# Reordered sums in the convolution loop and one image fewer in the DRAM round trip of a convolution with batch norm

## The chip, the cores and the metric

One core of one Trainium2 chip runs the whole program. The metric is device time in microseconds (us) of one launch. The kernel before took 1618.82 us, the median of 3 runs (1618.82 to 1619.4).

## The reference

```python
x: (32, 256, 28, 28) float32
xp  = log_pooling(x)            # 12 fixed averages (2 radii x 6 angles) over a 9x9 neighbourhood, laid out 4x3
out = conv(xp, w_conv1, stride (4, 3)) + conv(x, w_center) + b_center
mean, var = out.mean((0, 2, 3)), out.var((0, 2, 3))
out = (out - mean) * rsqrt(var + 1e-5) * gamma + beta
return relu(out + x)
```

The mean and the variance run over all 32 images, so nothing can be finished until every image has been convolved.

## The kernel before

The 256 channels lie as 128 partitions by two halves (c = 0, 1 of the input, o = 0, 1 of the output). An image of y (the convolution's result) is 128 x 1568 float32, 784 KB. Each image goes through two steps s = 2 * image + c. A step makes, on VectorE (DVE), differences of columns, box sums, and "pooled" sums from them. All products are made in three parts (high by high, low by high, high by low): ScalarE (ACT) copies a rounded high part, DVE subtracts it to get the low part (`lo_of_sums`, `lo_of_shifted`, `lo_of_pooled`), and TensorE (PE) multiplies. `inner_split` holds the parts of the inner sums and `pooled_split` those of the three pooled pairs. There is one buffer of each.

The DVE program of a step, in its written order (each engine runs its own program in order):

1. `differences`, which writes the source of `inner_split`. ACT then makes the high parts (`split_inner`).
2. at c = 0 `take_middle` of the image before, which puts the middle products into `y_stage`.
3. `lo_of_sums`, which waits for ACT and which PE waits for at the start of its step (`inner_lo_ready`).
4. `three_columns` (L467, row <- row, x_pad, then row3v <- row), which waits for `row2_ready`.
5. `lo_of_shifted`, `boxes`, at c = 0 `take_y` of the image before (it waits for PE to have finished that image), `first_sum`, `second_sum`, `lo_of_pooled` 0, `third_sum`, `lo_of_pooled` 1 and 2.

`row2` is a sum of two shifted reads of `x_wide`, made by DMAs. SP's queue (L285) loads the first operand as soon as `second_sum` of the step before has freed the buffer. POOL (L248) waits for it to land and issues a DMA that adds the second operand. `ends` is made the same way behind it, and `third_sum` waits for it. In SP's program the store of the last image's y (`y_stage` to `y_dram`, L315) stands behind the two loads at c = 0.

In the very first step SP issues, in this order: x, the first part of the weights, the first operand of `row2`, the second part of the weights (the outer taps); then it waits for the finished `row2`, and then come the first operand of `ends`, the x of c = 1 and the other weights.

The statistics use a pivot near the mean. In image 1 DVE makes it from image 0 with four `bn_stats`, two `bn_aggr` and a product (`make_pivot`). From then on ACT's `measure` takes two sums per half of each image, with the pivot as bias.

The last phase reuses the 191 KB per partition of phase-1 buffers as 30 places of 784 KB. Slot d = 0 is `y_stage` and `x_pad`; slot d > 0 is place 2d - 2 for y and place 2d - 1 for x, so 16 slots and 2 rounds. `tail_image(round_, d)` says which image a slot holds. The image in `y_stage` (LAST = 31) is never stored. All others are stored and loaded again. SP loads the places of round 0 as their old contents die: place 0 before image LAST - 1, places 1 and 2 before image LAST, places 3 to 6 once the y of image LAST - 1 is saved (`y_saved`), 7 to 11 once PE is through c = 0 of the last image, 12 to 21 once the last low parts exist, and so on. Per slot DVE scales and adds x (L710), ACT applies the relu (L459) and issues the store (L462). In round 1 SP and POOL load y and x into a slot once its store has landed.

Of the kernel before, what the change touches and what calls it, by code (L numbers as in the profile page):

```python
# [7 lines left out]
def conv_bn_relu_program(nc, x, x_wide, w_raw, b_center, gamma, beta, out, y_dram):  # L8
# [57 lines left out]
    with ctx:  # L66
        def sb(name, size, dt=F32):
            return ctx.enter_context(nc.sbuf_tensor(name, [P, size], dt))
# [68 lines left out]
        ALL_PLACES = 2 * (SLOTS - 1)  # L137

        def tail_image(round_, d):
            return LAST if round_ == d == 0 else SLOTS * round_ + d - 1  # L140

        def y_slot(d):
            return y_stage[:, :] if d == 0 else view(phase2, 2 * (d - 1) * PLACE, (1, PLACE))
# [8 lines left out]
                return view(x_pad, 2 * H, (X_PAD, CH), (1, HW))  # L152
            return view(phase2, (2 * d - 1) * PLACE, (HW, CH), (1, HW))

        pivot_stats = sb("pivot_stats", CH * 2 * 6)
        pivot_moments = sb("pivot_moments", CH * 2)
        minus_pivot = sb("minus_pivot", CH)
        sums = sb("sums", 2 * CH * IMAGES)
        totals = sb("totals", 2 * CH)
# [118 lines left out]
        def _(sp):  # L278
# [5 lines left out]
            def begin_sum(image, c, buf, n_columns, begun):  # L284
                sp.dma_start(view(buf, 0, (1, n_columns * TALL_PITCH)),  # L285
                             x_wide[bass.ds(image, 1), :, c, 0:n_columns * TALL_PITCH]
                             .rearrange("n p f -> p (n f)")).then_inc(begun, 16)
# [15 lines left out]
            def image_steps(image, first=False, last=False):  # L303
                for c in range(CH):
                    if not last:
                        sp.wait_ge(row3_ready, CH * image + c + 1)
                        sp.wait_ge(v_ready, CH * image + c + 1)
                        load_x(image + 1, c)
                    if c == 0:
                        begin_sums(image, 1)  # L310
                    elif not last:
                        begin_sums(image + 1, 0)
                    if c == 0 and not first:
                        sp.wait_ge(y_ready, CH * image + FREE)
                        sp.dma_start(y_dram[bass.ds(image - 1, 1)].rearrange("n p f -> p (n f)"),  # L315
                                     y_stage[:, :]).then_inc(y_saved, 16)
# [6 lines left out]
                    .then_inc(tail_loaded[d], 16)  # L323

            def load_places(first, end):
                for k in range(first, min(end, ALL_PLACES)):
                    (load_tail_x if k % 2 else load_tail_y)(0, 1 + k // 2)

            load_x(0, 0)
            load_weights(0, 0)  # L330
            begin_sum(0, 0, row2, W + 3, row2_begun)
            load_weights(0, 1)
            sp.wait_ge(row2_ready, 16)
            begin_sum(0, 0, ends, W, ends_begun)
            load_x(0, 1)
            load_weights(1, 0)
            load_weights(1, 1)
# [11 lines left out]
            load_places(1, 3)  # L349
            image_steps(LAST, last=True)  # L350

            sp.wait_ge(y_saved, 16 * LAST)
            load_places(3, AFTER_STAGE)
            sp.wait_ge(pooled_done, PAIRS * (CH * IMAGES - 1))
            load_places(AFTER_STAGE, AFTER_FIRST)
# [17 lines left out]
        def _(act):  # L373
# [28 lines left out]
            def copy_middle(image):  # L402
# [3 lines left out]
                for m in range(2):  # L406
                    nc.scalar.activation(view(m_copy, m * CH * HALF, (HALF, CH), (H, U), (1, H)),
                                         view(acc, (MBANK + CH * m) * BANK, (BANK, CH), (1, U), (U, H)), ACT.Copy)\
                        .then_inc(m_copied, 1)

            def measure(image, o):
                act.wait_ge(y_ready, CH * image + o + 1 + FREE)
                act.wait_ge(pivot_ready, 1)
                for kind, function in enumerate((ACT.Identity, ACT.Square)):
                    wait_from_one(act, y_measured, MOMENTS * image + KINDS * o + kind)
                    nc.scalar.activation(view(m_copy, 0, (1, HW)), view(y_stage, o * HW, (1, HW)), function,  # L416
                                         bias=minus_pivot[:, o:o + 1],
                                         accum_out=sums[:, bass.ds((kind * CH + o) * IMAGES + image, 1)])\
                        .then_inc(y_measured, 1)

            def image_steps(image, first=False, second=False):
                for c in range(CH):
                    s = CH * image + c
                    if c == 0 and not first:
                        copy_middle(image - 1)
                    split_inner(s)
                    if c == 1 and not first and not second:
                        measure(image - 1, 1)
                    if first:
                        split_weights(c, range(len(GROUPS)))  # L430
                        act.wait_ge(warmed_up, 1)
                    for j in range(PAIRS):
                        split_pooled(s, j)
                        if second and c == 1 and j > 0:
                            measure(image - 1, j - 1)
                    if c == 0 and not first and not second:
                        measure(image - 1, 0)

            act.sem_inc(m_copied, FREE)
# [2 lines left out]
            act.wait_ge(zeroed, ZEROED)  # L442
            image_steps(0, first=True)
            image_steps(1, second=True)
            with act.Fori(2, IMAGES) as image:
                image_steps(image)
            copy_middle(LAST)
            for o in range(CH):
                measure(LAST, o)
# [16 lines left out]
        def _(dve):  # L466
# [47 lines left out]

            every_other_column = (2 * H, U), (1, H)

            def take_middle(image):

                dve.wait_ge(m_copied, 2 * image + 2 + FREE)
                wait_from_one(dve, y_saved, 16 * image)  # L520
                wait_from_one(dve, y_measured, MOMENTS * image)
                m1, m2 = (view(m_copy, m * CH * HALF, (HALF, CH), (H, U), (1, H)) for m in range(2))
                add(view(y_stage, 0, (HW, CH), *every_other_column), m2, m1)
                sub(view(y_stage, H, (HW, CH), *every_other_column), m1, m2).then_inc(middle_taken, 1)

            def take_y(image):
                dve.wait_ge(pooled_done, PAIRS * CH * (image + 1))
                dve.wait_ge(middle_taken, image + 1 + FREE)
                for o in range(CH):
                    y = view(y_stage, o * HW, (H, 2), (2 * H, U), (1, H))  # L530
                    add(y, view(acc, 2 * o * BANK, (BANK, 2), (H, U), (1, H)), y).then_inc(y_ready, 1)

            def make_pivot():
                dve.wait_ge(y_ready, CH + FREE)
                for o in range(CH):
                    for half in range(2):
                        link(nc.vector.bn_stats(pivot_stats[:, (2 * o + half) * 6:(2 * o + half + 1) * 6],
                                                y_stage[:, o * HW + half * HALF:o * HW + (half + 1) * HALF]))
                for o in range(CH):
                    link(nc.vector.bn_aggr(pivot_moments[:, 2 * o:2 * o + 2],  # L540
                                           pivot_stats[:, 12 * o:12 * o + 12]))
                nc.vector.tensor_scalar(minus_pivot[:, :], view(pivot_moments, 0, (2, CH)), -1.0, None, ALU.mult)\
                    .then_inc(pivot_ready, 1)


            def pooled_place(s, j, first, *dims):
# [103 lines left out]
            def image_steps(image, second=False):  # L650
                for c in range(CH):
                    s = CH * image + c
                    differences(image, c)
                    if c == 0:
                        take_middle(image - 1)
                    lo_of_sums(s)
                    three_columns(image, c)
                    lo_of_shifted(s)
                    if second and c == 0:
                        take_y(image - 1)  # L660
                    boxes(s)
                    if not second and c == 0:
                        take_y(image - 1)
                    first_sum(s)
                    second_sum(s)
                    lo_of_pooled(s, 0)
                    if second and c == 1:
                        make_pivot()
                    third_sum(s)
                    lo_of_pooled(s, 1)  # L670
                    lo_of_pooled(s, 2)
# [3 lines left out]
            dve.wait_ge(zeroed, ZEROED)  # L675
            first_image()
            image_steps(1, second=True)
            with dve.Fori(2, IMAGES) as image:
                image_steps(image)
            take_middle(LAST)  # L680
            take_y(LAST)

# [4 lines left out]
            link(sub(var[:, :], totals[:, CH:2 * CH], square[:, :]))  # L687
            nc.vector.tensor_scalar(var[:, :], var[:, :], 0.0, EPS, ALU.max, ALU.add).then_inc(var_ready, 1)
            dve.wait_ge(params_loaded, 48)
            dve.wait_ge(pivot_ready, 1)  # L690
            link(sub(mean[:, :], totals[:, 0:CH], minus_pivot[:, :]))
            link(add(mean[:, :], mean[:, :], bias[:, :]))
            link(sub(bn_shift[:, :], bias[:, :], mean[:, :]))
# [10 lines left out]

            for round_ in range(ROUNDS):
                for d in range(SLOTS):
                    wait_from_one(dve, tail_loaded[d], 16 * round_ + 32 * (d > 0))
                    wait_from_one(dve, tail_x_loaded[d], 16 * round_)
                    for o in range(CH):
                        nc.vector.scalar_tensor_tensor(  # L710
                            out=x_slot(d, o), in0=y_slot(d)[:, o * HW:(o + 1) * HW],
                            scalar=bn_scale[:, o:o + 1], in1=x_slot(d, o), op0=ALU.mult, op1=ALU.add)\
                            .then_inc(scaled, 1)
# [108 lines left out]
```

## Time and profile before

| | |
|---|---|
| median of 3 runs | 1618.82 us |
| profiled execution, its own time | 1618.86 us |
| span in the profile, first to last instruction | 1617.2 us |
| TensorE matmul busy | 1461.5 us (90%), 8518 instructions |
| DVE busy | 1443.0 us (89%), 1327 instructions |
| ACT busy | 658.6 us (41%) |
| HBM read / written | 218.07 MB / 50.58 MB |

The page divides the span into 40 slices of 40.4 us. TensorE is full until slice 36 and does nothing after. The DMA engines are between four and seven tenths busy until there, and full to the end. The kernel so has two parts, a convolution paced by the compute engines and a last phase paced by bytes, and a change has to be read in each of them.

### The profile page before, as it was taken

How to read it: one execution, taken by the hardware profiler on the slowest of the kernel's cores; microseconds unless marked ns; L12 is line 12 of the kernel's file. 1: busy time of each engine (PE TensorE's matmuls, PEld its weight loads, DVE VectorE, ACT ScalarE, POOL GpSimd, SP SyncE). 2: the span in 40 equal slices, each digit the busy share in tenths (PEclk: the TensorE clock that was granted, in tenths of full speed). 3: DMA queues.
4: the chain of work that ended last, by engine and by line, in shares of the span. 5: the costliest groups of instructions: out<-in, count | busy, mean ns of one | idle time of the engine just before them, and what ended most of it. 6: DMA issues, size and time to landing. Idle time of an engine off the chain costs nothing.

```text
span 1617.2 us, 22814 instructions
## 1 busy us (share of the span) xinstructions
PE 1461.5 (90%) x8518; PEld 1458.7 (90%) x8518; DVE 1443.0 (89%) x1327; ACT 658.6 (41%) x721; POOL 121.0 (7%) x160
## 2 busy tenths in 40 slices
PE   9999999999999999999999999999999999993000
PEld 9899999999999999999999999999999999993000
DVE  8999999999999999999999999999999999996432
ACT  3334444444333444434343344433434344444432
POOL 1000000000000000000000000000000000000000
PEclk9999999999999999999999999999999999996555
DMA  7355555565455555555545555455554566579999
GB/s 222 88 133 140 144 129 129 131 147 131 122 120 134 147 137 128 127 133 140 131 113 123 145 146 136 125 127 139 137 126 110 132 147 158 155 237 424 425 425 402
DMA packets 65352, 268.76 MB, mean 166 GB/s; under 512 B 7616, under 2 KB 7616, under 8 KB 65344
## 3 DMA queue, kind: packets, MB, share of 16 engines
q1 hardware_dynamic: 39744, 160.53, 30.3%
q0 software_dynamic: 20736, 82.45, 25.7%
q10 hardware_dynamic: 4864, 25.69, 3.8%
q14 instruction: 6, 0.05, 0.0%
q8 instruction: 2, 0.03, 0.0%
HBM read 218.07 MB, written 50.58 MB: 166 GB/s over the span
## 4 chain that ended last, share of the span: by engine, by line
PE 83%; DVE 5%; DMA 4%; ACTq 3%; ACT 3%; issue 1%; SPq 0%; DVEq 0%; POOLq 0%
PE acc L724 28%; PE acc L725 28%; PE acc L723 28%; ACTq L462 3%; ACT phase L459 2%; DMA phase<-y_dram 2%; DVE phase L467 1%; DMA ends<-x_wide 1%; DVE pooled_split L468 1%; DMA row<-x_wide 1%; DMA out<-phase 1%; ACT m_copy L416 0%; DVE y_stage L467 0%; DVE inner_split L468 0%; DVE row L467 0%
## 5 line engine op out<-in xcount | busy, mean ns | idle before, releaser
L398 ACT ACTIVATE pooled_split<-phase 128x1456 fp32r<-128x1456 f32 x192 | 274.1, 1428 | 637.7 <-DVE phase L467 637.2
L468 DVE TENSOR_TENSOR pooled_split<-phase,pooled_split 128x1456 fp32r<-128x1456 f32 x192 | 315.1, 1668 | 0.3 <-ACT pooled_split L398 0.3
L723 PE MATMUL acc<-pooled_split,w_first 128*128 128x364 f32 x768 | 252.3, 329 | 1.5 <-DVE pooled_split L468 1.4
L724 PE MATMUL acc<-pooled_split,w_first 128*128 128x364 f32 x768 | 252.9, 329 | 0.0
L725 PE MATMUL acc<-pooled_split,w_first 128*128 128x364 f32 x768 | 252.8, 329 | 0.0
L725 PE MATMUL acc<-pooled_split,w_outer 128*128 128x364 f32 x768 | 252.7, 329 | 0.0
L723 PE MATMUL acc<-pooled_split,w_outer 128*128 128x364 f32 x768 | 252.1, 328 | 0.5 <-DVE pooled_split L468 0.5
L724 PE MATMUL acc<-pooled_split,w_outer 128*128 128x364 f32 x768 | 252.5, 329 | 0.0
L723 PE MATMUL acc<-inner_split,w_inner 128*128 128x392 f32 (+1 forms) x640 | 216.4, 338 | 3.0 <-DVE w_inner L510 3.0
L723 PE MATMUL acc<-inner_split,w_first 128*128 128x392 f32 (+1 forms) x640 | 217.8, 340 | 0.7 <-DVE inner_split L468 0.5
L725 PE MATMUL acc<-inner_split,w_inner 128*128 128x392 f32 (+1 forms) x640 | 217.3, 340 | 0.0
L724 PE MATMUL acc<-inner_split,w_inner 128*128 128x392 f32 (+1 forms) x640 | 217.3, 339 | 0.0
L724 PE MATMUL acc<-inner_split,w_first 128*128 128x392 f32 (+1 forms) x640 | 216.4, 338 | 0.0
L725 PE MATMUL acc<-inner_split,w_first 128*128 128x392 f32 (+1 forms) x640 | 215.5, 337 | 0.0
L467 DVE TENSOR_TENSOR phase<-box,row 128x1456 f32<-128x1456 f32 x128 | 208.1, 1667 | 0.0
L389 ACT ACTIVATE inner_split<-phase 128x1568 fp32r<-128x1568 f32 x64 | 97.1, 1518 | 208.3 <-DVE phase L467 208.3
L468 DVE TENSOR_TENSOR inner_split<-phase,inner_split 128x1568 fp32r<-128x1568 f32 x64 | 114.4, 1788 | 49.0 <-ACT inner_split L389 49.0
L723 PEld LDWEIGHTS acc<-pooled_split,w_first 128*128 128x128 f32 x768 | 144.4, 188 | 2.5 <-DVE pooled_split L468 2.5
L723 PEld LDWEIGHTS acc<-pooled_split,w_outer 128*128 128x128 f32 x768 | 144.2, 188 | 0.8 <-DVE pooled_split L468 0.8
L724 PEld LDWEIGHTS acc<-pooled_split,w_outer 128*128 128x128 f32 x768 | 144.5, 188 | 0.0
L725 PEld LDWEIGHTS acc<-pooled_split,w_outer 128*128 128x128 f32 x768 | 144.4, 188 | 0.0
L724 PEld LDWEIGHTS acc<-pooled_split,w_first 128*128 128x128 f32 x768 | 144.3, 188 | 0.0
(82 smaller groups left out, 2222.6 us busy)
## 6 DMA issues: line engine op xcount, KB each, us to landing
row<-x_wide SPq DMA_DIRECT2D x64, 558.0 KB, 3.7
row<-x_wide POOLq DMA_DIRECT2D x64, 558.0 KB, 7.5
ends<-x_wide SPq DMA_DIRECT2D x64, 504.0 KB, 3.9
ends<-x_wide POOLq DMA_DIRECT2D x64, 504.0 KB, 6.5
x_pad<-x SPq DMA_DIRECT2D x64, 392.0 KB, 3.1
y_dram<-y_stage SPq DMA_DIRECT2D x31, 784.0 KB, 5.5
phase<-y_dram SPq DMA_DIRECT2D x30, 784.0 KB, 23.6
out<-phase ACTq DMA_DIRECT2D x30, 784.0 KB, 33.3
```

Source lines behind the costliest of these rows:

```text
L389: nc.scalar.activation(view(inner_split, 0, (1, SD)), view(phase2, INNER_LOW, (1, SD)), ACT.Copy)\
L398: nc.scalar.activation(view(pooled_split, 2 * j * PAIR, (1, PAIR)), view(phase2, POOLED_LOW + 2 * j * PAIR, (1, PAIR)), ACT.Copy)\
L459: nc.scalar.activation(x_slot(d, o), x_slot(d, o), ACT.Relu, bias=bn_shift[:, o:o + 1]).then_inc(relu_done, 1)
L462: act.dma_start(out[tail_image(round_, d)].rearrange("p c w h -> p c (w h)"), x_slot_whole(d)).then_inc(stored[d], 16)
L467: add = lambda out_, a, b: nc.vector.tensor_tensor(out_, a, b, ALU.add)
L468: sub = lambda out_, a, b: nc.vector.tensor_tensor(out_, a, b, ALU.subtract)
L723: nc.tensor.matmul(place, hi_w, hi_in, start=start, stop=False)
L724: nc.tensor.matmul(place, lo_w, hi_in, start=False, stop=False)
L725: return nc.tensor.matmul(place, hi_w, lo_in, start=False, stop=stop)
```

## The change

- **Steps with c = 1**, in every image but the first: `three_columns` stands ahead of `lo_of_sums`. At c = 0 the order stays.
- **First step**: SP issues the first operand of `ends` ahead of its wait for `row2`, and the second part of the weights behind that wait.
- **Pivot**: made by ACT with two passes over `y_stage` (identity scaled by -1/784, with the running sum kept) behind the pooled parts of c = 0 of image 1. DVE's `make_pivot` is gone, and image 1 is measured in the same positions as every later image.
- **Image LAST - 1**: its y is finished in place 0 instead of `y_stage`. It is neither stored nor loaded. Slot 1 of round 0 holds it, and image 0 goes to slot 15 of round 1. SP no longer waits for that store ahead of places 3 to 6.
- The image loops of DVE and ACT end one image earlier, and the last image is written out.

```diff
         def tail_image(round_, d):
-            return LAST if round_ == d == 0 else SLOTS * round_ + d - 1
+            if d == 0 and round_ == 0:
+                return LAST
+            if d == 1 and round_ == 0:
+                return LAST - 1
+            return 0 if SLOTS * round_ + d == LAST else SLOTS * round_ + d - 1
...
-                    if c == 0 and not first:
+                    if c == 0 and not first and not last:
                         sp.wait_ge(y_ready, CH * image + FREE)
                         sp.dma_start(y_dram[...], y_stage[:, :]).then_inc(y_saved, 16)
...
-                for k in range(first, min(end, ALL_PLACES)):
+                for k in range(max(first, 1), min(end, ALL_PLACES)):
...
             begin_sum(0, 0, row2, W + 3, row2_begun)
+            begin_sum(0, 0, ends, W, ends_begun)
+            sp.wait_ge(row2_ready, 16)
             load_weights(0, 1)
-            sp.wait_ge(row2_ready, 16)
-            begin_sum(0, 0, ends, W, ends_begun)
             load_x(0, 1)
...
-            sp.wait_ge(y_saved, 16 * LAST)
+            sp.wait_ge(y_saved, 16 * (LAST - 1))
             load_places(3, AFTER_STAGE)
...
+            def make_pivot():            # on ACT
+                for o in range(CH):
+                    act.wait_ge(y_ready, o + 1 + FREE)
+                    wait_from_one(act, pivot_ready, o)
+                    nc.scalar.activation(view(m_copy, 0, (1, HW)), view(y_stage, o * HW, (1, HW)), ACT.Identity,
+                                         scale=-1.0 / HW, accum_out=minus_pivot[:, o:o + 1])\
+                        .then_inc(pivot_ready, 1)
...
+            def y_place(image, first, *dims):
+                if isinstance(image, int) and image == LAST - 1:
+                    return view(phase2, first, *dims)
+                return view(y_stage, first, *dims)
...
                     if c == 0:
                         take_middle(image - 1)
-                    lo_of_sums(s)
-                    three_columns(image, c)
+                        lo_of_sums(s)
+                        three_columns(image, c)
+                    else:
+                        three_columns(image, c)
+                        lo_of_sums(s)
                     lo_of_shifted(s)
...
-                    if second and c == 1:
-                        make_pivot()
...
-            with dve.Fori(2, IMAGES) as image:
+            with dve.Fori(2, LAST) as image:
                 image_steps(image)
+            image_steps(LAST)
```

## Rows read from the trace of the kernel before

**Rows 1.** The page: busy time of TensorE, and what the DMAs moved in 40 slices.

```profile
PE 1461.5 (90%) x8518; PEld 1458.7 (90%) x8518; DVE 1443.0 (89%) x1327; ACT 658.6 (41%) x721; POOL 121.0 (7%) x160
GB/s 222 88 133 140 144 129 129 131 147 131 122 120 134 147 137 128 127 133 140 131 113 123 145 146 136 125 127 139 137 126 110 132 147 158 155 237 424 425 425 402
```

**Rows 2.** Waits: who waited for whom, us in total, times, longest.

```profile
DVE inner_split L468 <- ACT inner_split L389: 49.0, 31, 1.6
DVE y_stage L467 <- PE acc L725: 33.0, 26, 10.5
```

**Rows 3.** Timeline, DVE, image 30: start, duration, [idle before <- releaser].

```profile
1378.47 0.97 DVE L467 TENSOR_TENSOR y_stage<-acc,y_stage 128x784 f32<-128x784 f32 x1 [0.94 <-PE acc L725]
...
1394.67 1.79 DVE L468 TENSOR_TENSOR inner_split<-phase,inner_split 128x1568 fp32r<-128x1568 f32 x1 [1.58 <-ACT inner_split L389]
1396.38 1.03 DVE L467 TENSOR_TENSOR row<-row,x_pad 128x840 f32<-128x840 f32 x1
```

**Rows 4.** Timeline, image 30: SP's store, POOL's row2 addition, PE's first product of c = 1.

```profile
1387.14 0.43 SPq L315 DMA_DIRECT2D y_dram<-y_stage  x1
...
1387.75 0.86 POOL L248 DMA_DIRECT2D row<-x_wide  x1 [19.58 <-DMA row<-x_wide]
...
1400.82 0.34 PE L723 MATMUL acc<-inner_split,w_inner 128*128 128x392 f32 x1
```

**Rows 5.** DMA issues, the addition at 1387.75: KB, us from issue to landing.

```profile
row<-x_wide POOLq DMA_DIRECT2D x1, 558.0 KB, 7.8
```

**Rows 6.** The same at c = 1 of image 2: POOL's issue, its landing, DVE's sum.

```profile
129.35 0.86 POOL L248 DMA_DIRECT2D row<-x_wide  x1 [17.38 <-DMA row<-x_wide]
...
row<-x_wide POOLq DMA_DIRECT2D x1, 558.0 KB, 8.0
...
137.75 1.03 DVE L467 TENSOR_TENSOR row<-row,x_pad 128x840 f32<-128x840 f32 x1
```

**Rows 7.** Timeline, DVE: `take_y` of images 1, 4 and 5.

```profile
119.86 1.85 DVE L467 TENSOR_TENSOR y_stage<-acc,y_stage 128x784 f32<-128x784 f32 x2
...
252.10 1.84 DVE L467 TENSOR_TENSOR y_stage<-acc,y_stage 128x784 f32<-128x784 f32 x2
...
296.55 1.86 DVE L467 TENSOR_TENSOR y_stage<-acc,y_stage 128x784 f32<-128x784 f32 x2 [0.31 <-PE acc L725]
```

**Rows 8.** Timeline, DVE, first step: the third sum.

```profile
27.53 1.74 DVE L467 TENSOR_TENSOR phase<-box,ends 128x728 f32<-128x728 f32 x2 [2.05 <-DMA ends<-x_wide]
```

**Rows 9.** Timeline, image 1: ACT's last pooled part of c = 0, DVE's pivot.

```profile
80.70 1.42 ACT L398 ACTIVATE pooled_split<-phase 128x1456 fp32r<-128x1456 f32 x1 [1.81 <-DVE phase L467]
...
100.03 2.37 DVE L537 BATCH_NORM_STATS2 pivot_stats<-y_stage 128x6 f32<-128x392 f32 x4
...
103.00 1.74 DVE L467 TENSOR_TENSOR phase<-box,ends 128x728 f32<-128x728 f32 x2
...
106.64 1.68 DVE L468 TENSOR_TENSOR pooled_split<-phase,pooled_split 128x1456 fp32r<-128x1456 f32 x1 [0.31 <-ACT pooled_split L398]
```

**Rows 10.** Timeline, image 31: DVE's sum at c = 0, SP's store and loads.

```profile
1418.83 1.03 DVE L467 TENSOR_TENSOR row<-row,x_pad 128x840 f32<-128x840 f32 x1 [1.16 <-DMA row<-x_wide]
...
1423.81 1.85 DVE L467 TENSOR_TENSOR y_stage<-acc,y_stage 128x784 f32<-128x784 f32 x2
...
1432.46 0.43 SPq L315 DMA_DIRECT2D y_dram<-y_stage  x1
1438.20 0.33 SPq L322 DMA_DIRECT2D phase<-x  x1
...
1456.36 0.33 SPq L319 DMA_DIRECT2D phase<-y_dram  x1
```

**Rows 11.** DMA issues: the addition at 1408.99, the load at 1456.36, and the first x.

```profile
row<-x_wide POOLq DMA_DIRECT2D x1, 558.0 KB, 9.8
...
phase<-y_dram SPq DMA_DIRECT2D x1, 784.0 KB, 6.5
...
x_pad<-x SPq DMA_DIRECT2D x1, 392.0 KB, 3.1
```

More of the change, by code:

```diff
@@ L153, in x_slot_whole @@
             return view(phase2, (2 * d - 1) * PLACE, (HW, CH), (1, HW))
-        pivot_stats = sb("pivot_stats", CH * 2 * 6)
-        pivot_moments = sb("pivot_moments", CH * 2)
         minus_pivot = sb("minus_pivot", CH)
@@ L409, in copy_middle @@
                         .then_inc(m_copied, 1)
+            def make_pivot():
[5 more added lines that the diff above has]
+                        .then_inc(pivot_ready, 1)
             def measure(image, o):
                 act.wait_ge(y_ready, CH * image + o + 1 + FREE)
-                act.wait_ge(pivot_ready, 1)
+                act.wait_ge(pivot_ready, CH)
                 for kind, function in enumerate((ACT.Identity, ACT.Square)):
                     wait_from_one(act, y_measured, MOMENTS * image + KINDS * o + kind)
-                    nc.scalar.activation(view(m_copy, 0, (1, HW)), view(y_stage, o * HW, (1, HW)), function,
+                    y = phase2 if isinstance(image, int) and image == LAST - 1 else y_stage
+                    nc.scalar.activation(view(m_copy, 0, (1, HW)), view(y, o * HW, (1, HW)), function,
                                          bias=minus_pivot[:, o:o + 1],
@@ L426, in image_steps @@
                     split_inner(s)
-                    if c == 1 and not first and not second:
+                    if c == 1 and not first:
                         measure(image - 1, 1)
@@ L433, in image_steps @@
                         split_pooled(s, j)
-                        if second and c == 1 and j > 0:
-                            measure(image - 1, j - 1)
-                    if c == 0 and not first and not second:
+                    if second and c == 0:
+                        make_pivot()
+                    if c == 0 and not first:
                         measure(image - 1, 0)
@@ L444, in _ @@
             image_steps(1, second=True)
-            with act.Fori(2, IMAGES) as image:
+            with act.Fori(2, LAST) as image:
                 image_steps(image)
+            image_steps(LAST)
             copy_middle(LAST)
@@ L515, in _ @@
             every_other_column = (2 * H, U), (1, H)
+            def y_place(image, first, *dims):
+                if isinstance(image, int) and image == LAST - 1:
+                    return view(phase2, first, *dims)
+                return view(y_stage, first, *dims)
             def take_middle(image):
                 dve.wait_ge(m_copied, 2 * image + 2 + FREE)
-                wait_from_one(dve, y_saved, 16 * image)
+                if isinstance(image, int) and image == LAST:
+                    dve.wait_ge(y_saved, 16 * (LAST - 1))
+                elif not (isinstance(image, int) and image == LAST - 1):
+                    wait_from_one(dve, y_saved, 16 * image)
                 wait_from_one(dve, y_measured, MOMENTS * image)
                 m1, m2 = (view(m_copy, m * CH * HALF, (HALF, CH), (H, U), (1, H)) for m in range(2))
-                add(view(y_stage, 0, (HW, CH), *every_other_column), m2, m1)
-                sub(view(y_stage, H, (HW, CH), *every_other_column), m1, m2).then_inc(middle_taken, 1)
+                add(y_place(image, 0, (HW, CH), *every_other_column), m2, m1)
+                sub(y_place(image, H, (HW, CH), *every_other_column), m1, m2).then_inc(middle_taken, 1)
             def take_y(image):
@@ L529, in take_y @@
                 for o in range(CH):
-                    y = view(y_stage, o * HW, (H, 2), (2 * H, U), (1, H))
+                    y = y_place(image, o * HW, (H, 2), (2 * H, U), (1, H))
                     add(y, view(acc, 2 * o * BANK, (BANK, 2), (H, U), (1, H)), y).then_inc(y_ready, 1)
[L533 to L543, printed above, removed]
             def pooled_place(s, j, first, *dims):
@@ L677, in _ @@
             image_steps(1, second=True)
-            with dve.Fori(2, IMAGES) as image:
+            with dve.Fori(2, LAST) as image:
                 image_steps(image)
+            image_steps(LAST)
             take_middle(LAST)
@@ L689, in _ @@
             dve.wait_ge(params_loaded, 48)
-            dve.wait_ge(pivot_ready, 1)
+            dve.wait_ge(pivot_ready, CH)
             link(sub(mean[:, :], totals[:, 0:CH], minus_pivot[:, :]))
@@ L706, in _ @@
                 for d in range(SLOTS):
-                    wait_from_one(dve, tail_loaded[d], 16 * round_ + 32 * (d > 0))
+                    wait_from_one(dve, tail_loaded[d], 16 * round_ + 32 * (d > 0) - 16 * (d == 1))
                     wait_from_one(dve, tail_x_loaded[d], 16 * round_)
```

## The prediction

> **What bounds the kernel now.** I read the page first, then the waits, then the timeline of one late image. On the page TensorE is busy for 1461.5 us, and the DMAs move 110 to 158 GB/s until slice 35, 237 in the next and 402 to 425 to the end [rows 1]. So two things are asked of each edit: whether it moves the convolution, which ends in slice 36, and whether it moves bytes in the stretch in which the DMAs are full. The waits say that DVE is nearly as loaded as TensorE. It waits for TensorE in only 26 places, and 31 times it waits 1.6 us for ACT's rounded copy [rows 2]. The timeline shows both in image 30: 0.94 us for TensorE ahead of `take_y`, 1.58 us for ACT ahead of `lo_of_sums` at c = 1 [rows 3]. `take_y` comes every 45.08 us from image 5 to image 29's end ((1378.47 - 296.55) / 24) [rows 3, 7]. That is TensorE's pace. From image 1 to 4 DVE didn't wait for TensorE and took 44.08 us an image ((252.10 - 119.86) / 3) [rows 7]; in the late images it is 45.08 - 0.94 = 44.14. I take 44.12 as DVE's own pace. **DVE has about 0.96 us an image to spare, and the change touches exactly that.**
>
> **The new order at c = 1.** It is meant to fill the 1.58 us wait with `three_columns`. But `three_columns` needs `row2`, and that arrives late. In image 30 POOL issues the addition at 1387.75 and it lands 7.8 us later, at 1395.55 [rows 4, 5]. The differences are done at about 1394.67 - 1.58 = 1393.09. DVE's sum started at 1396.38, so it had 0.83 us of margin [rows 3]. In image 2 it is 129.35 + 8.0 = 137.35 against 137.75, a margin of 0.40 [rows 6]. I read all 29 images from 2 to 30 this way, and the mean margin is 0.575 us. Moved ahead, the sum can start only that much earlier (less 0.04 us for the release). The 1.71 us of `lo_of_sums` (1396.38 - 1394.67), which lay inside the wait for the addition, now stands behind it. The chain that feeds the addition (`second_sum`, SP's load, POOL, landing) hangs on DVE's own work a fixed distance ahead, so it doesn't get faster. DVE then takes 44.12 + 1.71 - 0.575 + 0.04 = **45.29 us an image against TensorE's 45.08**: it becomes the bound, by 0.21 us an image. What is queued behind DVE's new wait is all of the step: both low parts, the boxes, and all that ACT, SP and POOL do from them. TensorE waits for the first low part, which it took up at 1400.82 when it had been there since 1396.4 [rows 3, 4], 4.4 us early. In the new order it would be there at 1396.38 - 0.79 + 2.0 (the two sums of `three_columns`, 1.03 us the first) + 1.71 = 1399.3, so 1.5 us of cover are left, and DVE's growing lag uses them up. Bounds: 44.08 and a landing 0.1 us earlier give 45.15, 44.14 and one 0.1 later give 45.41. Over 29 images that is +2.0 to +9.6 us, +6.1 at my value.
>
> **First step.** DVE waits 2.05 us for `ends` [rows 8]. The load of `ends` now goes out behind that of `row2`, some 12 us earlier, and its addition right behind `row2`'s on POOL, so the wait should go: -2.05 us for DVE. The outer weights go out about 12 us later instead. They cover themselves if they land before ACT's first pooled copy; if not, they give the 2.05 back. Range -2.05 to 0; I take -2.05, as these weights are 768 KB and head SP's queue when it wakes.
>
> **Pivot.** DVE loses 103.00 - 100.03 = 2.97 us of work and a 0.31 us wait for ACT, whose measuring stood in the way: -3.28 us [rows 9]. ACT gets two passes (about 1 us each) and measures c = 0 behind them. It ends its last pooled copy of c = 0 at 82.1 and has nothing to do for some 5 us, so about 4.3 us of passes fit. Cost 0. DVE paces from there, so both savings count.
>
> **DVE's chain to the last image.** `take_y` of image 1: 119.86 - 2.05 - 3.28 + 1.17 (the new order in image 1) = 115.70. 29 images of 45.29 lead to 1429.1. At c = 0 of the last image the addition is 1.16 us late because two loads of places go out ahead of it [rows 10]. Before, that fell into the time to spare; now it counts: 1430.3 against 1423.81 [rows 10], a shift of **+6.5 us**. All later releases hang on DVE, so the DMA phase begins that much later.
>
> **Bytes.** One store and one load of 784 KB are gone. The load (place 0) lay before the full stretch and is worth nothing. The store lay at its start, 1432.46 [rows 10]. It is worth 0.803 MB / 425 GB/s = **-1.9 us** [rows 1]. Slot 1 needs no y, and image 0 in the last slot needs what image 30 needed: 0. The bound from below is 0 and from above 3.8, if both counted.
>
> **What the missing wait lets loose.** SP's wait for that store held places 3 to 6 back from 1432.46 to 1438.20 [rows 10]. Now four loads go out at once, ahead of the last `row2` addition. With one store ahead the addition lands in 7.8 us, with two loads in 9.8 [rows 5, 11]. With four I take 10.8, between 9.8 and 13.8 (2 us for each more). In times of before, it is then issued at 1432.46 + 0.61 = 1433.07 [rows 4, 10], lands at 1443.9 instead of letting the sum start at 1441.7 (1396.38 + 45.34), and with 1.71 us of `lo_of_sums` behind it the last low parts are 3.9 us later: places 12 and up are released at 1460.3 instead of 1456.36. The load released there landed 6.5 us later, at 1462.9, behind others [rows 10, 11]; without the store the queue would bring it at 1461.0. But a load of 784 KB needs at least 3.1 + 0.9 = 4.0 us [rows 11] and so lands at 1464.3. The DMAs stand idle for **+3.3 us** (range 0 to 6).
>
> The Trainium skill ("DMA: Bandwidth & Descriptors", Queues, rings and completion order) says that each DMA engine takes turns between the queues' rings packet by packet. By that rule the POOL queue's addition gets its turns however many of SP's loads are queued, the landing would stay near the 9.8 us of the two-load case, and the idle time would be 2.3 us and not 3.3. The one-store and two-load rows differ by 2.0 us for 1.9 us of bytes and don't decide it.
>
> **The sum**, against the profiled execution's own 1618.86 us (its span of 1617.2 and 1.7 around it; the median of the runs shown is 1618.82): 1618.86 + 6.5 - 1.9 + 3.3 = **1626.8 us**, 0.5% slower.
>
> **Rivals.**
> - *The reorder pays and TensorE stays the bound.* If the addition at c = 1 lands early enough that DVE stays under 45.08 us, the convolution gains at its start alone, about 2.05 us, and the DMAs 1.9: 1618.86 - 2.05 - 1.9 = 1614.9 us, 0.2% faster, if the DMAs don't stand idle, and 1618.2 if they do for 3.3 us. It decides where the landing at c = 1 comes 0.2 us earlier than read. Against it: the 29 landings have a mean margin of 0.575 us, and it would take 0.8. For it: single images have that (image 30: 0.83 [rows 3 to 5]).
> - *A draw.* DVE's pace is 45.15 and the DMAs stand idle for 1 us: +2.4 - 1.9 + 1 = 1620.4, within 1615.6 to 1622.1. For it: 0.1 us of landing is 2.9 us of time.
> - *Worse.* Landings grow by 0.2 us and four loads hold the addition for 13.8 us: +12 - 1.9 + 6 = 1635.
> - *The tail edit does nothing.* If other DMAs hide the store, the -1.9 falls away: 1628.7. It lies inside the forecast's case.
>
> **How the numbers follow.** A difference of 0.2% is about what a measurement of this kernel can tell from none. Forecast (1622.1 to 1632.5) 0.62; reorder pays 0.17, of which 0.03 end within 0.2%; draw 0.17; worse 0.04. The range takes in the first three nearly whole: 1614.5 to 1632.5. Faster 0.14, same 0.20, slower 0.66.
>
> **What would show it.** Right: DVE waits at L467 row <- row, x_pad for the DMA 31 times for some 2.8 us each and no more for ACT at c = 1; the spacing of `take_y` is 45.2 to 45.4 us; TensorE has some 25 short waits for DVE's `inner_split`; DVE's waits for TensorE at `take_y` are gone but the last; no pivot and no wait at 27.5; DMA idle near the release of places 12 and up. Wrong: a spacing of 45.08 with waits for TensorE left; a landing of the c = 1 addition well under 7.8 us; first pooled copy of ACT late behind the outer weights.

## The result, and the profile after

The changed kernel takes **1626.26 us**, the median of 6 runs (1623.81 to 1628.43), against 1619.09 (1618.82 to 1619.53) for the kernel before on the same chips: a ratio of 1.0040, 95% interval 1.0029 to 1.0051. The forecast was 1626.8. The profiled execution has a span of 1625.0 us against 1617.2.

The page of the changed kernel: busy time, and GB/s in 40 slices.

```profile
PE 1466.1 (90%) x8518; PEld 1460.2 (90%) x8518; DVE 1438.1 (88%) x1320; ACT 660.3 (41%) x725; POOL 121.3 (7%) x160
GB/s 221 95 126 147 137 136 124 127 147 137 123 113 131 147 137 127 126 133 147 130 119 120 135 146 135 125 124 139 141 127 111 129 143 140 157 243 380 425 424 405
```

DVE has 4.9 us less to do than before and the kernel is slower all the same. The full stretch of the DMAs starts later: slice 37 moves 380 GB/s and not 424 [rows 1]. The waits say why.

```profile
DVE row L481 <- DMA row<-x_wide: 89.2, 32, 5.1
...
DVE y_stage L481 <- PE acc L738: 10.5, 2, 10.2
PEld acc L736 <- DVE inner_split L482: 10.3, 12, 3.7
```

The 31 waits for ACT are gone, and so are the waits for TensorE at `take_y`, 33.0 us in 26 places before [rows 2]: two are left, one of them at the very end. In their place DVE waits 32 times for the `row2` addition. Without the longest (5.07 us) and the one at c = 0 of the last image (1.06) that is (89.2 - 5.07 - 1.06) / 30 = 2.77 us each, where the wait for ACT took 1.58. And TensorE now waits for DVE. Image 30 on the timeline, with the landing of its addition (issued at 1392.82):

```profile
1400.89 1.03 DVE L481 TENSOR_TENSOR row<-row,x_pad 128x840 f32<-128x840 f32 x1 [2.79 <-DMA row<-x_wide]
...
1402.94 1.78 DVE L482 TENSOR_TENSOR inner_split<-phase,inner_split 128x1568 fp32r<-128x1568 f32 x1
...
row<-x_wide POOLq DMA_DIRECT2D x1, 558.0 KB, 8.0
```

The addition landed at about 1400.8 and DVE started right behind it; `lo_of_sums` stands behind the sums. `take_y` of images 1, 29 and 30, the lines that answer to [rows 3], [rows 7] and [rows 10]:

```profile
116.01 1.86 DVE L481 TENSOR_TENSOR y_stage<-acc,y_stage 128x784 f32<-128x784 f32 x2 [0.32 <-PE acc L738]
...
1383.49 1.85 DVE L481 TENSOR_TENSOR y_stage<-acc,y_stage 128x784 f32<-128x784 f32 x2
...
1429.93 1.85 DVE L481 TENSOR_TENSOR phase<-acc,phase 128x784 f32<-128x784 f32 x2
```

(1383.49 - 116.01) / 28 = **45.27 us an image**, against the 45.08 that the kernel before kept from image 5 on. The last image, DVE's and SP's timeline and the last addition's landing (issued at 1439.27):

```profile
1438.58 0.43 SPq L325 DMA_DIRECT2D phase<-x  x1
...
1449.60 1.03 DVE L481 TENSOR_TENSOR row<-row,x_pad 128x840 f32<-128x840 f32 x1 [5.07 <-DMA row<-x_wide]
...
1465.97 0.33 SPq L322 DMA_DIRECT2D phase<-y_dram  x1
...
row<-x_wide POOLq DMA_DIRECT2D x1, 558.0 KB, 10.2
```

The four loads that no longer wait for a store go out from 1438.58. Two are issued ahead of the addition (1438.58 and 1439.06) and two behind it (1439.53 and 1440.42), and the addition takes 10.2 us. Places 12 and up are released at 1465.97. That is 36.0 us behind `take_y` of image 30, against 1456.36 - 1423.81 = 32.6 before [rows 10]. The windows of 1 us there, with TensorE, PEld, DVE, ACT, POOL, granted clock, DMA share and GB/s:

```profile
1463.00:1464.00 1.00, 1.00 (x8) 1.00 (x7) 1.00 (x1) 1.00 (x1) 0.00 (x0) 1.00 0.84 351
1464.00:1465.00 1.00, 1.00 (x8) 1.00 (x7) 1.00 (x2) 1.00 (x3) 0.00 (x0) 1.00 0.00 0
1465.00:1466.00 1.00, 1.00 (x7) 1.00 (x7) 1.00 (x2) 0.66 (x1) 0.00 (x0) 1.00 0.00 0
1466.00:1467.00 1.00, 1.00 (x8) 1.00 (x7) 1.00 (x2) 0.00 (x0) 0.00 (x0) 1.00 0.32 44
1467.00:1468.00 1.00, 1.00 (x8) 1.00 (x7) 0.72 (x1) 0.00 (x0) 0.00 (x0) 1.00 0.61 125
```

The DMAs lose 0.16 + 1 + 1 + 0.68 + 0.39 = 3.2 us of a stretch that must be full. The kernel before has no such gap: its DMAs move 425 GB/s around its release at 1456.36.

A measure that splits each span in two helps from here on: **the lead** is the start of `take_y` of image 30, and **the tail** is the rest of the span. A kernel's lead shows the convolution's pace, its tail the DMA phase. Both are of the profiled execution. The kernel before took 1618.94 us beside e1 to e4, 1618.99 beside e5, e6, e8 and e9, and 1618.56 beside e7; the ratios are to these. A ratio is estimated from all runs of both kernels and can differ by 0.0005 from the quotient of the medians.

| kernel | lead | tail | median | ratio to before, 95% interval |
|---|---|---|---|---|
| before | 1423.8 | 193.4 | 1619.09 | |
| changed | 1429.9 | 195.1 | 1626.26 | 1.0040 (1.0029 to 1.0051) |
| e1 changed, old order | 1419.7 | 193.2 | 1614.62 | 0.9973 (0.9962 to 0.9983) |
| e2 before, new order alone | 1436.7 | 193.3 | 1631.56 | 1.0077 (1.0063 to 1.0091) |
| e3 changed, late store | 1421.1 | 195.0 | 1617.78 | 0.9993 (0.9984 to 1.0002) |
| e4 changed, late loads | 1431.1 | 193.4 | 1626.75 | 1.0043 (1.0030 to 1.0057) |
| e5 before, `ends` first alone | 1422.7 | 193.4 | 1616.76 | 0.9987 (0.9978 to 0.9996) |
| e6 old order, late loads | 1419.9 | 192.5 | 1613.99 | 0.9968 (0.9956 to 0.9980) |
| e7 late store, late loads | 1419.9 | 192.0 | 1614.28 | 0.9974 (0.9963 to 0.9984) |
| e8 before, pivot on ACT alone | 1421.5 | 193.1 | 1617.07 | 0.9987 (0.9978 to 0.9996) |
| e9 old order, early loads | 1419.1 | 192.4 | 1613.15 | 0.9963 (0.9950 to 0.9977) |

### The profile page after: what moved, and what is told of

It reads as the page before. It is cut to its first block, busy times and chain, and to the rows that moved or that the text cites. A ratio compares the mean times of both kernels' runs of the same rounds, so it can differ in the third digit from the quotient of the medians.

```text
span 1625.0 us, 22771 instructions
## 1 busy us (share of the span) xinstructions
PE 1466.1 (90%) x8518; PEld 1460.2 (90%) x8518; DVE 1438.1 (88%) x1320; ACT 660.3 (41%) x725; POOL 121.3 (7%) x160
## 4 chain that ended last, share of the span: by engine, by line
DVE 37%; DMA 19%; PE 18%; issue 16%; ACT 4%; ACTq 4%; DVEq 1%; POOLq 0%; SPq 0%
DMA row<-x_wide 19%; DVE phase L481 11%; DVE inner_split L482 7%; PE acc L736 6%; PE acc L737 6%; PE acc L738 6%; DVE box L481 4%; ACTq L476 4%; ACT phase L473 3%; DVE row L481 3%; DVE y_stage L481 3%; DVE pooled_split L482 3%; DVE d L482 2%; DVE phase L482 1%; DVE y_stage L482 1%
## 5 line engine op out<-in xcount | busy, mean ns | idle before, releaser
L481 DVE TENSOR_TENSOR row<-row,x_pad 128x840 f32<-128x840 f32 x64 | 66.0, 1031 | 89.2 <-DMA row<-x_wide 89.2
```

Source lines behind the costliest of these rows:

```text
L481: add = lambda out_, a, b: nc.vector.tensor_tensor(out_, a, b, ALU.add)
```

## The experiments

The theory is that of the prediction: the new order puts `lo_of_sums` behind a DMA that lands late. Its main rival is that something else in the change costs the time.

**e1, the old order back in the changed kernel.**

```diff
                     if c == 0:
                         take_middle(image - 1)
-                        lo_of_sums(s)
-                        three_columns(image, c)
-                    else:
-                        three_columns(image, c)
-                        lo_of_sums(s)
+                    lo_of_sums(s)
+                    three_columns(image, c)
```

> The changed kernel with lo_of_sums ahead of three_columns again at c = 1; all else as changed. Theory (the new order makes DVE the bound because row2 lands late): the spacing of take_y goes back to 45.08 us with waits for TensorE of some 0.9 us, DVE waits for ACT 1.58 us at c = 1. TensorE ends image 1 some 3.5 us earlier than in the kernel before, the store saves 1.9, and the DMAs' idle time shrinks from 3 us to some 1.6, because the last low parts no longer stand behind a sum: 1615 us (1613 to 1618). Rival (the loss comes from something else in the change, such as the written-out last image or the pivot on ACT): it stays at 1624 to 1628 us.

Measured 1614.62 us. The waits of this kernel:

```profile
DVE inner_split L482 <- ACT inner_split L392: 49.1, 31, 1.6
...
DVE y_stage L481 <- PE acc L735: 30.7, 26, 8.5
```

The 31 waits for ACT are back, and so are those for TensorE; the spacing is 45.08 us again. One edit is worth 11.6 us, more than the whole change costs. The rest of the change is a gain of 0.27%. The idle time of the DMAs isn't gone with the order: places 12 and up are released at 1453.93, 34.3 us behind `take_y` of image 30, where it was 32.6 before, and the 6 us from 1452 on move 282 GB/s.

**e2, the new order alone in the kernel before** (the same lines, the other way round).

> The kernel before with three_columns ahead of lo_of_sums at c = 1, and nothing else. Theory: DVE takes 45.27 us an image from image 1 on, without the 2.05 and 3.28 us that the changed kernel saves at its start: take_y of image 30 comes at 119.9 + 1.2 + 29 * 45.27 + 1.2 = 1435 instead of 1423.8, so 1630 us (1627 to 1634). Rival (the new order is harmless alone): 1619 us.

Measured 1631.56 us, 0.8% slower than before. Its waits:

```profile
DVE row L467 <- DMA row<-x_wide: 87.4, 32, 3.5
...
PEld acc L726 <- DVE inner_split L468: 12.1, 17, 2.7
```

The spacing is (1390.12 - 122.11) / 28 = 45.29 us. The new order costs 12.6 us here and 11.6 in the changed kernel, so it doesn't need the other edits to do harm. e1 and e2 together leave the rival nothing.

**e3, the store of y moved behind the addition**, to test that it is the landing which sets the pace.

```diff
                         load_x(image + 1, c)
+                    if c == 1 and not first and not last:
+                        sp.wait_ge(y_ready, CH * image + FREE)
+                        sp.dma_start(y_dram[...], y_stage[:, :]).then_inc(y_saved, 16)
                     if c == 0:
                         begin_sums(image, 1)
                     elif not last:
                         begin_sums(image + 1, 0)
-                    if c == 0 and not first and not last:
-                        sp.wait_ge(y_ready, CH * image + FREE)
-                        sp.dma_start(y_dram[...], y_stage[:, :]).then_inc(y_saved, 16)
```

> The changed kernel with SP's store of the last image's y moved from c = 0, where it goes out just ahead of POOL's row2 addition for c = 1, to c = 1 behind the load of the next x. The new order at c = 1 stays. Theory (the landing of the addition sets DVE's pace, and 1.5 us of it is the store ahead of it): the landing at c = 1 falls from 7.7 us to the 6.2 us of c = 0, DVE's wait from 2.75 to some 1.3 us, DVE's own pace to 43.8 us, and TensorE is the bound again at 45.08: 1616 us (1614 to 1619), the 3 us of idle DMAs being left. Rival (the landing doesn't depend on the store): the pace stays at 45.27 us and the time at 1624 to 1628 us.

Measured 1617.78 us. Waits, DVE's sum in image 30 and the landing of its addition (issued at 1384.85):

```profile
DVE row L481 <- DMA row<-x_wide: 49.8, 32, 5.0
...
DVE y_stage L481 <- PE acc L738: 34.7, 28, 8.6
...
1391.59 1.03 DVE L481 TENSOR_TENSOR row<-row,x_pad 128x840 f32<-128x840 f32 x1 [1.54 <-DMA row<-x_wide]
...
row<-x_wide POOLq DMA_DIRECT2D x1, 558.0 KB, 6.7
```

The mean landing at c = 1 (images 2 to 30) falls from 7.82 to 6.50 us, the wait with it, and TensorE is the bound again at 45.08 us, with the new order in place. So the new order costs this much because the addition lands when it does, and 1.3 us of that is the store ahead of it. It still gains nothing: the time is 1.8 us over what was expected and 3.2 over e1, which has the old order. The lead is 1.4 us longer than in e1. One part of that is a wait of 1.07 us of TensorE for the low part of c = 1 in image 1, which e1 doesn't have. The tail, 195.0, keeps all that the changed kernel lost there.

**e4, the four loads held back in the changed kernel.**

```diff
             sp.wait_ge(y_saved, 16 * (LAST - 1))
+            sp.wait_ge(row2_ready, 16 * CH * IMAGES)
             load_places(3, AFTER_STAGE)
```

> The changed kernel in which SP waits for the last row2 addition ahead of places 3 to 6. Theory (these four loads hold the addition up for some 4 us, and the last low parts with it): the addition lands in 6.3 us instead of 10.2, TensorE's wait of 3.4 us there and the 3 us without DMA traffic ahead of places 12 and up go; about 1 us of DMA time is lost ahead of the four loads: 1624 us, 2 us under the changed kernel (1622 to 1625). Rival (the idle time lies elsewhere or is made up later): no difference, or slower by the 4 us that the loads start later.

Measured 1626.75 us, no readable difference: a miss of the number. In the trace the mechanism does what the theory says:

```profile
1448.04 1.03 DVE L482 TENSOR_TENSOR row<-row,x_pad 128x840 f32<-128x840 f32 x1 [2.35 <-DMA row<-x_wide]
...
row<-x_wide POOLq DMA_DIRECT2D x1, 558.0 KB, 7.5
```

The addition lands in 7.5 us instead of 10.2, the DMAs no longer stand idle at the release of places 12 and up (1464.42), and the tail is 193.4 us instead of 195.1. But the profiled execution's lead was 1.2 us longer than the changed kernel's: DVE waited 2.80 us an image for `row2` and not 2.77, which is 0.9 us over 29 images, and 1.42 us at c = 0 of the last image where it was 1.06. Both waits lie ahead of the edit. Besides, the six and five runs of the two kernels spread over 4.6 and 4.2 us. By its time alone e4 fits its rival (no difference) as well. This needed a kernel that TensorE paces.

**e7, the same wait in e3.**

> The changed kernel with the late store of y (new order at c = 1 kept, TensorE the bound) and with SP waiting for the last row2 addition ahead of places 3 to 6. The late loads gave no readable difference in the changed kernel itself, whose time spreads by 4 us from run to run. Here the spread is 3 us and the comparison is with 1617.8 us. Theory (four loads ahead of the last addition cost 3 us of idle DMAs under the new order): the addition lands in 7 us instead of 10.1, the idle time near 1456 us goes, and the time from take_y of image 30 to the end falls from 195.1 to some 193.3 us: 1616.0 us (1615.3 to 1616.8). Rival (the idle time is made up by the earlier start of the loads): 1617.8 us or more.

Measured 1614.28 us, a ratio of 0.9974 against e3's 0.9993, and a tail of 192.0 us against 195.0. The addition lands in 6.1 us:

```profile
1435.28 1.03 DVE L482 TENSOR_TENSOR row<-row,x_pad 128x840 f32<-128x840 f32 x1 [0.77 <-DMA row<-x_wide]
```

The gain is nearly twice what was expected. 3.0 us of it is the tail in these two executions. The same edit took 1.7 us off in e4, where the addition landed in 7.5 us and not in 6.1, so 3.0 is the upper of two readings. The lead is 1.2 us shorter too, and that isn't the edit's: `take_y` of image 1 came 0.64 us earlier (113.72 against 114.36), both kernels kept 45.08 us from image 2 to 29, and the remaining 0.5 us fell at c = 0 of the last image, where the addition landed in 9.5 us and not in 10.1. The landings were shorter throughout (6.2 us against 6.4 at c = 0). Why they were is open; the two kernels ran on different chips and at different times.

**e6, the same wait with the old order.**

> The changed kernel with the old order at c = 1, and with SP waiting for the last row2 addition ahead of places 3 to 6. Without the spread of the new order a difference of 1 us can be read. Theory: the addition lands in 7.5 us instead of 10.0, the last low parts come 1.5 us earlier, and the 1.5 us with little traffic near 1454 us go, but the loads start 8 us later, so the DMAs may still be at work on places 3 to 11 when places 12 and up are released; then only the total of bytes counts: 1614 us (1613 to 1615), a draw or up to 1 us better than 1614.6. Rival (the loads' early start is worth its bytes): slower, 1616 to 1618 us.

Measured 1613.99 us against 1614.62. That is what was expected, though the runs of the two kernels overlap. The last addition landed in 6.6 us instead of 10.0. With the old order the last low parts don't stand behind the sum, so less is lost by the four loads: 0.8 us of tail, where it was 1.7 to 3.0 with the new one.

**e5, `ends` first, alone; e8, the pivot on ACT, alone**, each in the kernel before and with the change's own lines.

```diff
-            load_weights(0, 1)
+            begin_sum(0, 0, ends, W, ends_begun)
             sp.wait_ge(row2_ready, 16)
-            begin_sum(0, 0, ends, W, ends_begun)
+            load_weights(0, 1)
```

> The kernel before with the new order of the first step's loads, and nothing else. Theory: DVE's wait of 2.05 us for ends goes, DVE and then TensorE are 2.05 us earlier from c = 1 of image 0 on, TensorE stays the bound and keeps it: 1616.9 us (1616.5 to 1617.5). Rival (the outer weights land too late or TensorE waits for something else in image 0 or 1): 1618 to 1619 us.

> The kernel before with the pivot made by ACT, and nothing else. Theory: DVE is 3.28 us earlier from image 1 on; only TensorE's two waits for DVE at the end of image 1 (0.8 us at 106.4 and 0.5 us at 115.1) go with it, the rest is time to spare for DVE: 1617.5 us (1617 to 1618). Rival (ACT's passes hold up split_inner at c = 1 of image 1, or the wait lay elsewhere): 1619 us or more.

Measured 1616.76 and 1617.07 us where the kernel before took 1618.99: -2.2 and -1.9 us. Together that is -4.1, and e1, which has both and the image that stays, is at -4.3. If the two add up, which no run tested, the image that stays in its place is worth about 0.2 us, and 0.9 with the loads held back (e6 is at -5.0). Both are within the spread of these kernels, 1.3 and 2.1 us from run to run. It fits that the store's 1.9 us are mostly given back by the loads let loose in its place: the release 1.7 us later in e1.

**e9, places 1 to 6 loaded early, with the old order.** Nothing else uses the memory of places 1 to 6 after the weights are split.

```diff
                         load_x(image + 1, c)
+                    place = CH * (image - LAST + 3) + c + 1 if isinstance(image, int) else 0
+                    if 1 <= place <= 6:
+                        load_places(place, place + 1)
...
-            with sp.Fori(1, LAST - 2) as image:
+            with sp.Fori(1, LAST - 3) as image:
                 image_steps(image)
-            image_steps(LAST - 2)
             sp.wait_ge(w_lo_ready, CH * len(GROUPS))
-            sp.wait_ge(y_saved, 16 * (LAST - 3))
-            load_places(0, 1)
+            sp.wait_ge(y_saved, 16 * (LAST - 5))
+            image_steps(LAST - 3)
+            image_steps(LAST - 2)
             image_steps(LAST - 1)
-            load_places(1, 3)
             image_steps(LAST, last=True)
...
-            load_places(3, AFTER_STAGE)
```

> The changed kernel with the old order at c = 1, and places 1 to 6 loaded one by one in images 28, 29 and 30, each behind the load of the next x, where the row2 addition has landed. No load stands in front of image 31's additions any more. Theory (what counts is when places 12 and up are released, and the bytes after that): the waits of 1.1 us at c = 0 and of the last c = 1 for row2 go, which brings the release some 2.5 to 3 us forward, and that is the gain: 1611.8 us (1611 to 1613). Rival (the end of the DMA phase is bytes from its start on, so four loads taken out of it are worth 4 * 1.9 us): 1607 us. Other rival (single early loads delay additions in images 28 to 30 and hold DVE up): no gain.

Measured **1613.15 us, the lowest median of all, 0.37% under the kernel before and 0.8% under the changed one**. The rival's 1607 is out: four loads (7.6 us of bytes) taken out of the full stretch gave 1.5 us. The other rival is out too: `take_y` kept 45.08 us, and the landings at c = 1 their mean of 7.84 us. The windows show what became of the rest:

```profile
1438.00:1442.00 4.00, 4.00 (x26) 4.00 (x25) 3.98 (x5) 0.00 (x0) 0.00 (x0) 1.00 0.00 0
...
1444.00:1453.00 9.00, 9.00 (x53) 9.00 (x53) 9.00 (x8) 5.35 (x5) 0.00 (x0) 1.00 1.01 416
1453.00:1454.00 1.00, 1.00 (x8) 1.00 (x7) 0.37 (x1) 0.00 (x0) 0.00 (x0) 1.00 0.83 157
```

The DMAs now stand idle before 1442, when nothing else may be loaded. The expected 2.8 us came out as 1.5 because places 12 and up were released 2.3 us earlier than in e1 (1451.63 against 1453.93), but the bytes of places 7 to 11 still flowed until 1453. From the release to the end it took 0.8 us longer than in e1, and 2.3 - 0.8 = 1.5.

## Why the prediction was right

| step | predicted | measured in the changed kernel |
|---|---|---|
| DVE's wait for `row2` at c = 1 | some 2.8 us, 31 times | 2.77 us, and 5.07 in the last |
| spacing of `take_y` | 45.29 us | 45.27 |
| first step | -2.05 us | `take_y` of image 0 at 68.28 and not 70.37: -2.09 |
| `take_y` of image 1 | 115.70 | 116.01 |
| `take_y` of image 30 | 1430.3 | 1429.93 |
| landing of the last addition | 10.8 us (9.8 to 13.8) | 10.2 |
| idle DMAs | +3.3 us | 3.2 |
| tail, store and idle time | -1.9 + 3.3 = +1.4 | +1.7 |
| span, against 1617.2 | +7.9 | +7.8 |

**What carried it.** One margin was read 29 times, 0.575 us between the landing of the addition and the sum that uses it. It says that a step moved ahead of a wait gains only what its own input is early by, and that the 1.71 us of work it passes then lies in the open. e1, e2 and e3 show this from three sides.

**What was luck.** Single terms were off by up to half a microsecond, and they cancelled: `take_y` of image 1 came 0.3 us late, the way from there to image 30 was 0.7 us shorter, and the tail was 0.3 us longer. The runs of the changed kernel spread over 4.6 us, so a hit within 0.5 us of the median says nothing about terms of this size. The profiled execution is 0.4 us above the median; by the medians the kernel is 7.2 us slower, and not 7.8 or the forecast 7.9. One row was read wrongly without harm: 110 to 158 GB/s until slice 35 leaves out the first two slices, which move 222 and 88 [rows 1].

**The covers held.** The outer weights came late for ACT, and the pivot's passes fitted. ACT's timeline:

```profile
19.04 1.58 ACT L387 ACTIVATE w_first<-w_stage 128x512 fp32r<-128x512 f32 x2 [5.93 <-DMA w_stage<-w_raw]
21.86 2.95 ACT L401 ACTIVATE pooled_split<-phase 128x1456 fp32r<-128x1456 f32 x2 [1.24 <-DVE phase L481]
...
79.95 0.84 ACT L419 ACTIVATE m_copy<-y_stage 128x784 f32<-128x784 f32 x1
...
84.99 1.52 ACT L392 ACTIVATE inner_split<-phase 128x1568 fp32r<-128x1568 f32 x1 [0.86 <-DVE phase L481]
```

ACT waited 5.93 us for the weights and still had 1.24 us left ahead of its first pooled copy. The four passes of the pivot and of c = 0 ended 0.86 us ahead of the next `split_inner`.

**What was a little off.** `take_y` of image 1 waited 0.32 us for TensorE, which the chain of DVE alone doesn't see: TensorE had itself been held up at c = 1 of image 1, by a wait for the low part (2.41 us on its timeline, 2.7 with the weight load), and then ran part of the time at the lower clock (the last section has the lines). I expected some 25 short waits of TensorE in the image loop; the records name 12 in all. Their size fits better than their number: 28 images of 0.19 us are 5.3 us, and the 12 hold 10.3 us, of which 2.7 and 3.7 are image 1 and the last and 3.9 the ten between. The store was taken as -1.9 us and the idle time as 3.3; only their sum is tested by the changed kernel. The windows read 3.2 for the idle time; taking it away was worth 3.0 us of tail in e3 against e7 and 1.7 in the changed kernel against e4.

**The rule on turns.** The two ends for the last landing were 9.8 us if the queues take turns and up to 13.8 if loads go first in line. Two loads ahead gave 9.5 to 10.1 us (c = 0 of the last image in all kernels but e9), four gave 10.2, 10.0 and 10.1 (the changed kernel, e1, e3). Two more loads cost about 0.3 us and not 4. That alone doesn't decide for turns, because the third and the fourth load are issued just behind the addition, and plain order of issue would give the same. The packets of the queues in the changed kernel say more (SP's queue is q1, POOL's q0: packets, MB, share of the DMA engines), from the addition's issue to 4.0 us behind it, and from there to its landing:

```profile
q1 hardware_dynamic: 281, 1.34, 94.8%
...
q0 software_dynamic: 162, 0.64, 51.8%
q1 hardware_dynamic: 216, 1.20, 51.8%
```

In the first 4.0 us no packet of the addition moved; in e6, with nothing ahead, its first came within 2 us. After that both queues had the engines for the same share of the time. That part agrees with the rule of the Trainium skill ("DMA: Bandwidth & Descriptors", Queues, rings and completion order). Why the addition didn't get its turns in the first 4 us is open.

## What to carry to other kernels

Before a step is moved ahead of a wait, look up when its own inputs arrive: it can gain no more than that margin, and everything it overtakes is then added behind it. Where two engines are within 1 us of each other over a loop, the spare time of the second is a budget, and each edit of a loop body has to be charged against it 30 times. In a phase bound by bytes, a removed transfer counts only if the queue never runs dry behind it; look for what releases the next ones.

## What the runs showed of the hardware

- A kernel that a DMA's landing paces seems to inherit its scatter. Single landings at c = 1 lie between 7.2 and 8.4 us, and the runs of the changed kernel spread over 4.6 us and those of e2 over 6.0. Those of e1, with the same DMAs behind a margin, spread over 0.7. No run separates this from other differences: e3, which TensorE paces, still spread over 3.4.
- A wait of 3.36 us of TensorE in the last image was followed by a stretch at the lower clock. Timeline and window (granted clock 0.61 of full speed over 4 us, so mostly the level of 1.2 GHz):

```profile
1453.49 0.45 PE L736 MATMUL acc<-inner_split,w_inner 128*128 128x392 f32 x1 [3.36 <-DVE inner_split L482]
...
1454.00:1458.00 4.00, 4.00 (x17) 4.00 (x16) 4.00 (x5) 0.02 (x1) 0.00 (x0) 0.61 1.02 427
```

No cost shows here: the DMAs moved 427 GB/s in this window and 422 in the next 4 us, and the release at 1465.97 hangs on DVE. The wait of 2.41 us in image 1 was followed by the same:

```profile
91.61 0.44 PE L736 MATMUL acc<-inner_split,w_inner 128*128 128x392 f32 x1 [2.41 <-DVE inner_split L482]
...
92.00:96.00 4.00, 4.00 (x17) 4.00 (x16) 4.00 (x5) 0.00 (x0) 0.00 (x0) 0.62 0.00 0
```

The waits of up to 0.8 us in the image loop left the clock at 1.00. In between, the wait's length alone doesn't tell: 1.85 us in image 0 of e1 was followed by 0.64 over the 4 us from 42.00, while 2.25 us in image 2 of e2 and 1.55 us in the last image of e3 left it at 1.00.
